# Gelu in place in PSUM, and its high and low parts made from there

## The reference

```python
for e in range(E):                       # 8 experts, each token uses 2 of them
    h = jax.nn.gelu(jnp.einsum('bsh,ih->bsi', x, w_up[e]), approximate=False)
    y = jnp.einsum('bsi,hi->bsh', h, w_down[e])
    out = out + sparse_w[..., e:e + 1] * y
...
x = x + 0.5 * _L0_ffn_ref(_layernorm(x, axis=-1), ...)
x = x + _L0_attn_ref(_layernorm(x, axis=-1), ...)
x = x + 0.5 * _L0_ffn_ref(_layernorm(x, axis=-1), ...)
```

## Time and profile before

| | us |
|---|---|
| median of 3 runs | 1236.83 |
| the runs | 1235.48 to 1241.78 |
| the profiled execution, its time | 1232.84 |
| its span, first to last instruction | 1231.0 |
| busy in the span: PE / DVE / ACT / POOL | 912.4 / 979.3 / 710.2 / 790.4 |
| first feed-forward's turns, about | 116 to 278 |
| attention, about | 280 to 1036 |
| second feed-forward's turns, about | 1037 to 1174 |
| POOL's last result scatter issued | 1191 |

### The profile page before, as it was taken

One profiled execution on the slowest core, in us unless ns is written; L12 is line 12 of the kernel. 1 busy time (PEld: TensorE's weight loads), 2 busy tenths in 40 slices (PEclk: granted clock), 3 DMA queues, 4 the chain that ended last, 5 costly groups with the idle time before them and its releaser, 6 DMA issues.

```text
span 1231.0 us, 32392 instructions
## 1 busy us (share of the span) xinstructions
PE 912.4 (74%) x12594; PEld 741.2 (60%) x12594; DVE 979.3 (80%) x2124; ACT 710.2 (58%) x1033; POOL 790.4 (64%) x665
## 2 busy tenths in 40 slices
PE   3302989777996897897897876888796886789910
PEld 2301988765775675675675655566574665679910
DVE  7887777896878899889899888778988866867724
ACT  2111867556775674674775664675674564657704
POOL 2087744825886676676675644888775575577755
PEclk9999999999998998998998998998997987889965
DMA  9332433429993000000000000000000001233233
GB/s 340 137 109 75 132 86 105 106 56 184 192 194 57 8 9 6 8 9 5 8 9 1 2 2 2 15 19 15 12 14 6 6 24 36 54 82 97 83 117 126
DMA packets 91778, 78.26 MB, mean 64 GB/s; under 512 B 7952, under 2 KB 81040, under 8 KB 91376
## 3 DMA queue, kind: packets, MB, share of 16 engines
q1 hardware_dynamic: 82272, 58.18, 20.2%
q0 software_dynamic: 8640, 17.78, 4.7%
q10 hardware_dynamic: 720, 0.23, 0.1%
HBM read 30.07 MB, written 46.09 MB: 62 GB/s over the span
## 4 chain that ended last, share of the span: by engine, by line
DVE 26%; POOL 26%; PE 24%; issue 14%; ACT 6%; DMA 3%; DVEq 0%; POOLq 0%; SPq 0%; ACTq 0%
POOL arena_a L1835 5%; DVE arena_b L1731 4%; POOL xs L784 4%; POOL arena_a L1817 4%; DVE arena_a L1689 3%; POOL xs L816 3%; PE bank L1493 3%; ACT arena_c L1605 3%; DVE arena_c L1727 2%; POOL arena_b L845 2%; PE bank L1417 2%; POOL arena_c L1839 2%; DVE xn_new L479 2%; PE bank L1419 2%; PE bank L1418 2%
## 5 line engine op out<-in xcount | busy, mean ns | idle before, releaser
L1835 POOL TENSOR_TENSOR arena_a<-arena_a 128x1024 f16<-128x1024 f32 x64 | 139.1, 2173 | 52.4 <-ACT arena_a L1605 51.5
L1817 POOL TENSOR_TENSOR arena_a<-arena_b,trig_rows 128x512 f32<-128x512 f32 x128 | 160.4, 1274 | 6.8 <-issue 6.8
L1605 ACT ACTIVATE arena_c<-arena_a 128x1024 f16<-128x1024 f32 x64 | 67.6, 1057 | 164.6 <-DVE arena_a L1689 164.6
L1714 DVE TENSOR_TENSOR arena_b<-bank,decay 128x512 f32<-128x512 f32 x128 | 82.4, 686 | 47.6 <-PE bank L1493 47.1
L1605 ACT ACTIVATE arena_b<-arena_b 128x512 f16<-128x512 f32 x128 | 78.3, 629 | 64.8 <-DVE arena_b L1714 64.8
L1332 POOL DMA_INDIRECT ys<-arena_b,row_at x78 | 85.2, 1092 | 35.8 <-issue 22.3
L997 ACT ACTIVATE arena_c<-bank,s_pre 128x1024 f32<-128x1024 f32 x46 | 51.2, 1114 | 94.9 <-PE bank L932 89.8
L1417 PE MATMUL bank<-wo_hi,arena_c 128*128 128x128 f16 x256 | 53.1, 238 | 69.9 <-DVE arena_c L1698 69.9
L816 POOL DMA_INDIRECT xs<-xhl,slot_idx x64 | 78.6, 1228 | 40.4 <-issue 40.4
L1838 POOL TENSOR_TENSOR arena_c<-arena_c 128x130 f16<-128x130 f32 x64 | 29.7, 464 | 111.3 <-ACT arena_c L1655 111.3
L1689 DVE SCALAR_TENSOR_TENSOR arena_a<-bank,trig_cols 128x512 f32<-128x512 f32 x128 | 82.4, 684 | 23.3 <-PE bank L1419 23.0
(11 more groups left out here) (320 smaller groups left out, 4260.0 us busy)
## 6 DMA issues: line engine op xcount, KB each, us to landing
xs<-blank SPq DMA_DIRECT2D x8, 2210.0 KB, 32.7
xs<-arena_c SPq DMA_DIRECT2D x2, 3072.0 KB, 18.2
arena_b<-xs SPq DMA_DIRECT2D x46, 128.0 KB
ys<-arena_b SPq DMA_DIRECT2D x46, 128.0 KB, 1.9
arena_b<-xs SPq DMA_DIRECT2D x39, 130.0 KB, 2.3
arena_a<-in_w_up SPq DMA_DIRECT2D x1, 2048.0 KB, 12.8
arena_b<-in_w_down SPq DMA_DIRECT2D x1, 2048.0 KB, 13.6
arena_a<-ys SPq DMA_DIRECT2D x4, 512.0 KB, 5.4
```

The costliest lines, as they stand in the source:

```text
L1605: nc.scalar.activation(dst, src, ACT.Copy, scale=scale).then_inc(done, 1)
L1714: i = nc.vector.tensor_tensor(probs[:, h * BLK:(h + 1) * BLK].rearrange("p (c i) -> p c i", c=TPB), ps_so[:, h, :].rearrange("p (c i) -> p ...
L1817: i = nc.gpsimd.tensor_tensor(q_trig[h], q_relu[h], trig_rows[:, bass.ds(u * BLK, BLK)], ALU.mult)
L1835: nc.gpsimd.tensor_tensor(q_lo, arena_a[:, 0:2 * BLK], q_hi, ALU.subtract).then_inc(a["q_lo_done"], 1)
```

## The change

Gelu writes over the two PSUM banks that it reads. `h32` is now a name for these banks, so that ACT makes the high part from PSUM, and DVE's `low` reads its first input from PSUM and its second (`h_hi`) from SBUF as before. `h32` is gone from `arena_c`, and `h_hi` and `h_lo` lie 2048 words lower there. Since the banks are needed until `low` has read them, PE's `up(G)` waits for `lo_done` of turn G - 2 and no longer for its `gelu_done`. ACT's wait for `lo_done` ahead of Gelu goes.

```diff
         take = carve(arena_c)
-        h32 = [take(PAIR * BLK) for _ in range(2)]
         h_hi = [take(PAIR * BLK, F16) for _ in range(4)]
         h_lo = [take(PAIR * BLK, F16) for _ in range(4)]
...
         ps_pre = [bank[0], bank[1]]
+        h32 = [ps[:, :, :].rearrange("p c t -> p (c t)") for ps in ps_pre]
...
             def up(G, at_e):
                 pe.wait_ge(f["x_copied"], G + 1)
                 if G > 1:
-                    pe.wait_ge(f["gelu_done"], G - 1)
+                    pe.wait_ge(f["lo_done"], G - 1)
...
                         act.wait_ge(f["up_done"], G + 1)
-                        if G > 1:
-                            act.wait_ge(f["lo_done"], G - 1)
-                        nc.scalar.activation(h32[G % 2], ps_pre[G % 2][:, :, :].rearrange("p c t -> p (c t)"), ACT.Gelu,
+                        nc.scalar.activation(h32[G % 2], h32[G % 2], ACT.Gelu,
                                              scale=s_pre[:, 0:1]).then_inc(f["gelu_done"], 1)
...
             def up(p):
                 G, at_e = HALVES_DONE + p, expert_of(p)
                 pe.wait_ge(f["x_copied"], G + 1)
-                pe.wait_ge(f["gelu_done"], G - 1)
+                pe.wait_ge(f["lo_done"], G - 1)
...
                 act.wait_ge(f["up_done"], G + 1)
-                act.wait_ge(f["lo_done"], G - 1)
-                nc.scalar.activation(h32[G % 2], ps_pre[G % 2][:, :, :].rearrange("p c t -> p (c t)"), ACT.Gelu,
+                nc.scalar.activation(h32[G % 2], h32[G % 2], ACT.Gelu,
                                      scale=s_pre[:, 0:1]).then_inc(f["gelu_done"], 1)
```

## The result

The changed kernel takes 1221.64 us in the median of 4 runs (1216.22 to 1231.13), the kernel before 1237.76 in the same comparison: ratio 0.9889, 95% interval 0.9858 to 0.9919. Another comparison, with 6 runs of the changed kernel, gave 1221.86 against 1234.9, ratio 0.9899 [0.9870, 0.9928]. The ratios are those that each comparison gives, with their intervals; they are not quotients of the two medians. By its ratio the gain is 13.7 us (10.0 to 17.6) in the first comparison and 12.5 us (8.9 to 16.1) in the second, where the medians lie 16.1 and 13.0 apart. Two executions of the kernel before, of 2362 and 4850 us, stand far outside all others and are in no ratio. The forecast was 1219 in a range of 1212 to 1233. The profiled execution of the changed kernel is one of 1220.5 us, with a span of 1218.7.

A forecast was written before the change was run, and what follows sets the result against it. Bounds: PE in undisturbed turns, late low parts beside POOL's adds, POOL in the second feed-forward. First feed-forward -5.6 and second -12.3 give -17.9 us, from the 1236.83 median to 1219, range 1212 to 1233.

The forecast's parts named there:

- The low part no longer shares the way: First feed-forward, turns 16 to 21: low parts at 1.28 us beside POOL's long adds, -5.8 us including clock effects.
- Durations: Each turn: low part stays 1.28 us, high part 1.11 for 1.15, Gelu in place at no extra cost.
- POOL in FF2: Second feed-forward: 86 scatters at 0.96 us without stretching, -13.6 us, POOL ending near 1178.7 with some 5 us of margin.
- Start of FF1: First feed-forward's start: `up(2)` waits for low part 0 and `down(0)` comes one `up` later, +1.3 us.
- The start of FF2: Second feed-forward's start: `down(0)` and all up to POOL's first row scatter come one `up` later, +1.3 us.
- Second half of FF1: First feed-forward, turns 30 to 45: DVE's waits for powers gone, -2.9; later `up`, +1.8; together -1.1 us.
- Attention unchanged: Attention, between the feed-forwards: starts 5.6 us earlier and is itself not changed.
- The step from the profiled execution to the median: Whole kernel: the median of the runs lies 4.0 us above the profiled execution, so 1236.83 - 17.9 = 1219 us.
- Rival 1: Both feed-forwards: low part still shares DVE's and POOL's way to SBUF, +5.3 us, 1242 us; chance 0.12.
- rival 2: Both feed-forwards: Gelu in place is slow, costing a second pass, about 1232 and up to 1242 us; chance 0.08.
- Rival 3: PE or buffers bound the second feed-forward early, or attention gives some back; half the gain, 1228 us; chance 0.14.
- rival 4: Whole kernel: more arrives through a faster Gelu into PSUM and fewer low clock stretches, 1213 us and below; chance 0.04.

The follow-up runs named there:

- before, again: The kernel before, unchanged, run and profiled once more; 1233.78 us, ratio to itself 0.9987.
- FF2 alone: Kernel before with the change in the second feed-forward only, the first as before; 1223.55 us, ratio 0.9892.
- waits alone: Kernel before with only `up` waiting for the low part of two turns before instead of Gelu, both feed-forwards; 1240.82 us against 1236.90, ratio 1.0032.
- adds cut short: Kernel before with POOL's two long adds (L394) cut to one column of each tile; 1232.27 us against 1237.14, ratio 0.9968.
- 0-13, 22-48 apart: Changed kernel with turns 0 to 13 and 22 to 48 working as before; 1217.05 us, ratio 0.9847; once more 1215.89 us, ratio 0.9848.
- changed, again: The changed kernel run and profiled once more; 1221.86 us against 1234.9, ratio 0.9899.
- operand alone: Kernel before plus the new `up` wait and the low part's first input from PSUM (values ahead of Gelu); Gelu still writes SBUF; 1222.32 us, ratio 0.9886.
- FF1 alone: Kernel before with the change in the first feed-forward only, the second as before; 1235.40 us, ratio 0.9979.
- 0-2, 46-48 apart: Changed kernel with turns 0 to 2 of each feed-forward working as before; 1218.57 us against 1237.14, ratio 0.9862.
- 0-2, 37-48 apart: Changed kernel with turns 0 to 2 and 37 to 48 working as before; 1218.38 us against 1237.14, ratio 0.9847.

## Why the prediction was right, and where it was not

By the table, the change is worth -2.0 us in FF1 (166.60 to 164.59, 165.28 to 163.25), nothing in attention, +1.26 at the start of FF2, and -14.3 on POOL (mean of 122.59 over the five profiles with the old FF2, less 108.33 over the eight with the new one): together -15.0 us. Measured were -16.1 and -13.0 by the medians, -13.7 and -12.5 by the ratios, and the forecast was -17.9, which lies outside both intervals. So the gain was forecast some 3 us too large. FF1 makes 3.6 us of that (-2.0 for -5.6), and FF2 gives 0.7 back (-13.0 for -12.3).

FF1 can be split at the low part of turn 22. Lengths in us, with TensorE's granted clock in the same stretch:

| low part of turn 3 to that of turn 22 | us | clock |
|---|---|---|
| before | 60.40 | 0.97 |
| before, again | 58.89 | 1.00 |
| FF2 alone; waits alone | 60.29; 61.25 | 0.97 |
| the nine with the new form in turns 14 to 21, or with the adds cut short | 54.59 each | 1.00 |

| low part of turn 22 to attention's first power | us | clock |
|---|---|---|
| old form there: before; FF2 alone; 0-13, 22-48 apart, again | 99.38; 99.43; 99.41 | 0.98 |
| old form there: before, again; adds cut short; 0-13, 22-48 apart | 99.58; 99.19; 99.59 | 0.97 |
| waits alone | 100.47 | 0.97 |
| new form there: changed, again; operand alone | 100.27; 100.37 | 0.97 |
| new form there: changed; FF1 alone | 101.60; 101.58 | 0.95 |
| new form there: 0-2, 46-48 apart | 102.84 | 0.93 |
| new form to turn 36: 0-2, 37-48 apart | 102.14 | 0.92 |

By the steps of the forecast:

- **The low part no longer shares the way.** Right. Low parts at 1.28 us beside the adds, all of the stall of turns 16 to 21 gone: from turn 3 to turn 22 the changed kernel takes 54.59 us, which is 19 turns of 2.87, and gains 5.81 us on the first profile of before, for -5.8 forecast. The operand-alone run shows that this one input does it, the short-adds run that the other side of it was the adds. But only 4.30 us of the 5.81 are the stall. Behind the long low parts of the first profile stands a stretch at 1.2 GHz (the forecast had it in its -5.8, as one `up` at that clock), and the second profile of before has none there and loses 1.51 us less. The window 176 to 186 us, in the first and in the second profile of before (columns as above; the clock is the third number from the end):

```profile
176.00:186.00 10.00, 10.00 (x119) 9.00 (x117) 6.55 (x11) 6.50 (x6) 0.00 (x0) 0.83 0.29 80
```

```profile
176.00:186.00 10.00, 9.73 (x140) 9.35 (x141) 7.94 (x13) 7.70 (x7) 0.00 (x0) 1.00 0.38 100
```

  Of the four profiles with the stall three have such a stretch between turns 3 and 22, of the nine without it none. What the first pair gains there by the clock it loses again behind turn 22, as the step on the second half says.
- **Durations.** Right: low part 1282 ns from PSUM in the operand-alone run and 1282 from SBUF in the short-adds run; high part 1.11 us; Gelu in place 1.09, no longer than into SBUF. The extra cycles that the Trainium skill gives for a PSUM source ("VectorE: DVE Perf Modes", The TRN2 errata) would have made an estimated 1.35 us of the low part; no run shows them.
- **POOL in FF2.** Right: 108.24 us for the 108 to 109 forecast, -13.84 for -13.6, ending at 1178.66 for 1178.7. Most of the forecast lived on this term. Its margin was foreseen too: the last `take_y` of the changed kernel starts at 1171.61, where "near 1170.5" was forecast, 4.8 us ahead of POOL's last pair at 1176.45, and it waits for PE, no longer for a scatter:

```profile
1171.61 0.61 DVE L1274 TENSOR_SCALAR arena_b<-bank,arena_b 128x128 f32<-128x128 f32 x2 [1.15 <-PE bank L1198]
```

  So of a further shortening of POOL's stretch some 5 us could arrive before PE bounds FF2 (an estimate from the 4.8 us; no run tries it).
- **Start of FF1.** Named rightly, a bit small: +1.58 us for +1.3. `up(2)` started 0.45 us after the end of low part 0 (120.89 + 1.28 to 122.62), not 0.13 us as `down(0)` did in the earlier trace rows. That is so wherever `up` waits for a low part: it starts 0.44 us behind the low part's end in five of its seven waits in the second half, and 0.50 and 0.53 us in the two others, while `down`, waiting at 273.00, starts 0.13 us behind. In the order of PE's instructions the wait of `up` stands on the first of three small instructions ahead of its matmul; that they take the other 0.31 us is the likely reason, and no run moves the wait. So the cover in an undisturbed turn was 0.62 - 0.44 = 0.18 us and not 0.49. It sufficed. The start of FF2 was +1.25 for +1.3.
- **Second half of FF1.** Wrong, the one step that failed: -1.1 forecast, +2.2 us measured in the first profiles (-4.67 to -2.45) and +0.7 in the second. The term of the sum that was mis-sized is the -2.9 for DVE's waits for powers. The waits did go, no DVE wait for a power is left in these turns, but going they were worth about nothing: the run with the waits alone and the one with the operand alone differ in the low part's operand only, which frees POOL's gathers, and take 100.47 and 100.37 us at the same clock (the new wait is in both; without it the gathers alone were not tried). The price of the new wait, forecast at +1.8, is 0.9 us by the same table (100.47 against 99.58 in the second profile of before, both at 0.97). Together that is +0.8 at equal clocks, as in the second profiles. The other 1.5 us of the first pair come with the clock, 0.98 before and 0.95 in the changed kernel. How the -2.9 is lost shows on PE's row of the changed kernel, where `up` waits for a low part, seven times for 7.9 us in all:

```profile
212.31 0.28 PE L930 MATMUL bank<-arena_b,wup_hi 128*128 128x256 f16 x1 [1.10 <-DVE arena_c L1020]
...
228.33 0.28 PE L930 MATMUL bank<-arena_b,wup_hi 128*128 128x256 f16 x1 [1.10 <-DVE arena_c L1020]
...
245.70 0.39 PE L930 MATMUL bank<-arena_b,wup_hi 128*128 128x256 f16 x1 [1.10 <-DVE arena_c L1020]
```

  and on DVE's row, where the earlier trace rows had the powers, in the waits of `take_y` for PE:

```profile
204.33 0.42 DVE L1027 COPY arena_b<-bank 128x256 f32<-128x256 f32 x1 [0.66 <-PE bank L947]
...
215.17 0.42 DVE L1027 COPY arena_b<-bank 128x256 f32<-128x256 f32 x1 [1.45 <-PE bank L947]
...
232.84 0.42 DVE L1027 COPY arena_b<-bank 128x256 f32<-128x256 f32 x1 [2.08 <-PE bank L947]
...
250.15 0.42 DVE L1027 COPY arena_b<-bank 128x256 f32<-128x256 f32 x1 [1.41 <-PE bank L947]
...
275.76 0.42 DVE L1027 COPY arena_b<-bank 128x256 f32<-128x256 f32 x1 [1.96 <-PE bank L947]
```

  The first row is an undisturbed turn's. What the other four have above its 0.66 us is 0.79, 1.42, 0.75 and 1.30, together 4.3 us, where the forecast had 1.8. In the second profile of the changed kernel, at the higher clock, the same waits have 2.5 us above 0.66. So DVE waits for PE instead of for powers; a wait that goes is a gain only if nothing else ends up in its place.
- **Attention unchanged.** Right, as far as a stretch can tell that varies by 6 us; it is not to be read from one pair of profiles.
- **The step from the profiled execution to the median.** The forecast added 4.0 us because the first profile lay that much under the median. The table gives most of it: attention in it was 2.7 us under the mean of 13 profiles. That step carried over to 1219. That the time came within 2.6 us of it although the gain was some 3 us too large owes something to luck: the medians of this comparison lie 16.1 us apart, where the stretches add up to 15.0 and the ratio gives 13.7.

Rival 1 is excluded by the low parts and scatters of the changed kernel and of the operand-alone run, rival 2 by Gelu's 1088 ns. Rival 3, only a part arrives, named PE or the buffers in FF2 and attention, and none of them came; what is missing is missing in FF1, which gains 2.0 us of 5.6 and stood in no rival. Of rival 4 the faster Gelu came, by 25 ns, and was off the path.

## What to carry to other kernels

A tuned kernel can lose time because two engines share a way to memory, and the page shows it only as a mean that is larger than the minimum of the same form. Ask which single operand makes the pair collide: here one DVE input moved to PSUM was the whole effect; the new wait was its price, and Gelu in place is what lets the low part find its input there. A buffer that is kept one step longer makes the producer wait for one consumer more; give it only the turns in which the collision happens, as in the kernel with turns 14 to 21 of FF1 and all but the first three of FF2, which kept the gain without the price (1215.9 against 1221.9 us; by the stretches of the two pairs of profiles, 3.0 us of it in FF1 and 1.4 us at the start of FF2).

A stretch that varies by 6 us from one execution to the next can hide or fake an effect of 2 us. Lay the code that was not changed side by side first, compare a stretch only with several profiles, and put the granted clock beside each: one slow stretch of the clock moved 1.5 us from one step of FF1 to the next.

## What the runs showed of the hardware

In three of the profiles whose FF2 has the low part with two SBUF inputs (before, before again, waits alone) the 94 scatters of FF2 were sorted by when they began. The 58 that began outside a low part took 0.95 to 1.04 us. Of the 36 that began inside one, 34 ended 0.83 or 0.84 us behind the low part's end, however early they had begun. So a scatter is held only if it begins inside the low part; one that began 0.11 us ahead of a low part (1114.55 in the run with the waits alone, the low part at 1114.66) took 0.95:

```profile
1114.55 0.95 POOL L1332 DMA_INDIRECT ys<-arena_b,row_at  x1 [0.30 <-issue]
```

```profile
1114.66 1.27 DVE L1267 SCALAR_TENSOR_TENSOR arena_c<-arena_c,s_h 128x1024 f16<-128x1024 f32 x1
```

With the first input in PSUM (changed kernel) the 35 that began inside a low part took 0.95 to 0.96. One scatter of that profile, outside any low part, took 1.41: it began inside another DVE instruction with two SBUF inputs, and ended 0.84 us behind that one's end (1050.85):

```profile
1050.17 0.68 DVE L529 SCALAR_TENSOR_TENSOR xsrc<-xn_new,xsrc 128x512 f16<-128x512 f32 x1
```

```profile
1050.28 1.41 POOL L1329 DMA_INDIRECT ys<-arena_b,row_at  x1 [0.30 <-issue]
```

POOL's long add and the low part exclude each other the same way, and there each holds the other: the low part took 4.87 us for 1.28, and the two adds, one of which had a low part ahead of it, 9.97 us together in the kernel before against 9.00 in the changed one.

The Trainium skill ("SBUF — State Buffer", Who interferes with whom) has the rule that a DVE instruction with two SBUF inputs contends with a GpSimd instruction that reads SBUF, and one with at most one such input, outside the 2-port modes, does not; the adds and the scatters here agree with it. The same section infers that `tensor_tensor` takes only the shared read interface while descriptor generation needs the write interface, and explains with it that such an instruction did not stall a DMA; the indirect DMAs that POOL issues here were held, 0.96 us becoming up to 2.01.

ScalarE was faster where PSUM took the place of SBUF: Gelu 1088 ns into its own bank and 1113 into SBUF, the high part 1114 ns from PSUM and 1148 from SBUF (changed kernel and operand-alone run).
